# Attention head loop: one head more of lookahead, with a third buffer for scores and probabilities

## The chip, the cores and the metric

The kernel runs on the 8 cores of one Trainium2 chip, each core with its own batch element. The metric is the device time in microseconds of the slowest core, as the median of timed runs.

## The reference

One transformer layer on x of shape (8, 2048, 1024) in float32; one batch element of 2048 rows goes to each core. The attention is local: rows are taken in blocks of 64, and each block attends to itself alone, with 8 heads of 128.

```python
q = (src @ Wq + bq).reshape(B, nb, bs, H, dk)      # nb = 32 blocks of bs = 64
k = (src @ Wk + bk).reshape(B, nb, bs, H, dk)
v = (src @ Wv + bv).reshape(B, nb, bs, H, dk)
scores = jnp.einsum('bnqhd,bnkhd->bhnqk', q, k) * dk ** (-0.5)
probs = jax.nn.softmax(scores, axis=-1)
out = jnp.einsum('bhnqk,bnkhd->bnqhd', probs, v).reshape(B, S, D)
x = x + (out @ Wo + bo)                            # src is layernorm(x)
h = jnp.square(jax.nn.relu(jnp.einsum('bsd,fd->bsf', layernorm(x), W_fc)))
y = jnp.einsum('bsf,df->bsd', h, W_proj)           # then 5 spike steps, added to x
```

## The kernel before

The program is written out by hand: `plan` holds a list of instructions for each engine, in the order in which the Python code appends them, and each engine runs its list in that order. A wait stands in the list ahead of the instruction that needs it and holds back all that is behind it on that engine.

The attention runs in four passes (p = 0 to 3, called first to fourth) over 512 rows each. A pass has three parts. First come the projections: TensorE makes q and k (lines 336 and 356, evicted by ScalarE) and v (line 375, evicted by VectorE at line 383). Then comes the head loop, and last the output projection (line 617), with the residual added on VectorE (line 636) and the transposes of the next pass's normalized rows between.

In the head loop one step h (0 to 7) belongs to one head, that is 8 blocks of 64 rows. A head goes through these functions:

- `scores(h)`: 8 small matmuls into half h % 2 of psC (TensorE, line 405).
- `softmax_pre(h)`: maximum and subtraction from psC into s_f32 (VectorE, lines 419 and 422).
- `exp_h(h)`: exponential in place (ScalarE, line 431).
- `softmax_post(h)`: sum, reciprocal and product into p_bf (VectorE, lines 441, 444, 447).
- `pt_h(h)`: two transposes of p_bf into half h % 2 of psD (TensorE, line 459).
- `ptev_h(h)`: copy of them into pt_bf (ScalarE, line 468).
- `pv_h(h)`: probabilities times v into psA or psB (TensorE, line 488).
- `attnev_h(h)`: eviction with bias into attn_sb (VectorE, line 506).

Behind each head's PV the same loop transposes the FFN weights, which the second half of the kernel reads back from memory. `w2_group` makes 8 transposes of W2 into half 0 of psD (line 541), VectorE copies them to w2stage buffer 0 (line 551), and SP stores them to w2scratch (line 561). `w1_group` makes 8 transposes of W1 into half 1 of psD (line 514), ScalarE copies them to w2stage buffer 1 (line 525) and issues the store to w1scratch (line 533). So each of the two streams has one stage buffer and waits, ahead of a copy, for its own store of the step before. GpSimd refills the W2 buffers with 512 KB (line 197) behind every odd step's W2 transposes, and a W1 buffer with 256 KB (line 218) behind the W1 transposes of each step. In steps 1 to 4 of passes one to three ScalarE also computes the sums for the next pass's layer norm (lines 246 and 250), in step 5 VectorE and ScalarE turn them into a scale, and in step 6 VectorE applies it (line 283).

psD is shared: `relD` holds for each half the eviction that must be over before the next writer may start. The last passes' ends are followed by the FFN (lines 815 and 849) in eight tiles of 256 rows.

The order of the loop before:

```python
for h in range(8):
    if h + 2 < 8:
        E_s = scores(h + 2); softmax_pre(h + 2, E_s); exp_h(h + 2)
    if h + 1 < 8:
        softmax_post(h + 1); pt_h(h + 1); ptev_h(h + 1)
    pv_h(h)
    attnev_h(h)
    ...
    w2_group(ci, h % 2)
    ...
    w1_group(fcw)
```

Ahead of it stand scores, softmax_pre and exp of heads 0 and 1, and softmax_post, pt and ptev of head 0.

Of the kernel before, what the change touches and what calls it, by code (L numbers as in the profile page):

```python
# [12 lines left out]
ACT = mybir.ActivationFunctionType  # L13
# [11 lines left out]
def build_nc():  # L25
# [36 lines left out]
             for i in range(2)]  # L62
    p_bf = [e(nc.sbuf_tensor(f"p_bf_{i}", [128, 256], BF16, side="right"))
            for i in range(2)]
    pt_bf = [e(nc.sbuf_tensor(f"pt_bf_{i}", [128, 256], BF16, side="right"))
             for i in range(2)]
    ident = e(nc.sbuf_tensor("ident", [128, 128], BF16, side="right"))
# [252 lines left out]
    for p in range(PA):  # L320
# [93 lines left out]
        def softmax_pre(h, E_s):  # L414
            sv = psC[:, (h % 2) * 512:(h % 2) * 512 + 256]
            g3 = sv.rearrange("p (g k) -> p g k", g=4)
            wait("ve", "pe", E_s)
            wait("ve", "ve", war["tta"])
            op("ve", lambda E, g3=g3: E.tensor_reduce(
                negmax[:, :4], g3, AX.X, ALU.max, negate=True), inc="ve")  # L420
            wait("ve", "ve", n["ve"])
            op("ve", lambda E, h=h, g3=g3: E.tensor_tensor(
                s_f32[h % 2][:].rearrange("p (g k) -> p g k", g=4), g3,
                negmax[:, :4].unsqueeze(2).broadcast_to([128, 4, 64]),
                ALU.add), inc="ve")
            E_tta[h] = n["ve"]
            war["tta"] = n["ve"]

        def exp_h(h):
            wait("se", "ve", E_tta[h])  # L430
            op("se", lambda E, h=h: E.activation(
                s_f32[h % 2][:], s_f32[h % 2][:], ACT.Exp), inc="se")
            E_exph[h] = n["se"]

        def softmax_post(h):
            wait("ve", "se", E_exph[h])
            wait("ve", "ve", war["p"])
            if h >= 2:
                wait("ve", "pe", E_pt[h - 2])
            g3 = s_f32[h % 2][:].rearrange("p (g k) -> p g k", g=4)  # L440
# [7 lines left out]
                p_bf[h % 2][:].rearrange("p (g k) -> p g k", g=4), g3,  # L448
# [5 lines left out]
        def pt_h(h):  # L454
# [3 lines left out]
            for t_ in range(2):  # L458
                op("pe", lambda E, h=h, t_=t_, base=base: E.transpose(  # L459
                    psD[:, base + t_ * 128:base + (t_ + 1) * 128],  # L460
                    p_bf[h % 2][:, t_ * 128:(t_ + 1) * 128], ident[:]),
# [3 lines left out]
        def ptev_h(h):  # L465
# [3 lines left out]
                pt_bf[h % 2][:], psD[:, base:base + 256]), inc="se")  # L469
# [3 lines left out]
        def pv_h(h):  # L473
# [7 lines left out]
            for bl in range(8):  # L481
# [11 lines left out]
                       pt_bf[h % 2][kb:kb + 64,  # L493
# [82 lines left out]
        ptev_h(0)  # L576
        for h in range(8):
            if h + 2 < 8:
                E_s = scores(h + 2)
                softmax_pre(h + 2, E_s)  # L580
                exp_h(h + 2)
            if h + 1 < 8:
                softmax_post(h + 1)
                pt_h(h + 1)
                ptev_h(h + 1)
# [419 lines left out]
```

How the kernel before makes its waits and increments, by code:

```python
    def wait(eng, sem, val):  # L117
        if val <= 0:
            return
        assert val <= n[sem], (eng, sem, val, n[sem])
        emit(eng, lambda E, sem=sem, val=val: E.wait_ge(S[sem], val))
# [1 line left out]
    def op(eng, build, inc=None):  # L123
        if inc is None:
            emit(eng, lambda E, b=build: b(E))
            return None
        n[inc] += 1
        emit(eng, lambda E, b=build, s=inc: b(E).then_inc(S[s], 1))
        return n[inc]
# [3 lines left out]
    def dma(eng, build):  # L133
        npool = {"sy": NSY, "gp": NGP, "se": NSE}[eng]
        pfx = {"sy": "qs", "gp": "qg", "se": "qe"}[eng]
        k = qidx[eng] % npool
        qidx[eng] += 1
        nm = f"{pfx}{k}"
        if n[nm] > 0:
            wait(eng, nm, n[nm])
        n[nm] += 16
        emit(eng, lambda E, b=build, nm=nm: b(E).then_inc(S[nm], 16))
        return (nm, n[nm])
```

## Time and profile before

| | us |
|---|---|
| median of the timed runs (2 runs) | 1159.28 |
| lowest and highest of them | 1158.76, 1159.81 |
| profiled execution, its own time | 1154.09 |
| its span on the slowest core | 1152.5 |
| spans of the 8 cores | 1140.6 to 1152.5 |
| busy in the span: TensorE, VectorE, ScalarE, GpSimd | 831.0, 491.6, 411.8, 254.6 |

The span runs from the first to the last instruction of the slowest core. The head loops of the four passes begin at 99, 222, 347 and 470 us and end, with the first output projection matmul, at 158, 283, 407 and 523 us; the FFN fills the span from about 540 us on. A busy share is an average over both halves of the kernel and does not tell what a change in the head loop is worth.

### The profile page before, as it was taken

What the parts mean: (1) busy time and instruction counts of PE and PEld (TensorE: products, weight loads), DVE (VectorE), ACT (ScalarE), POOL (GpSimd) and SP (SyncE); (2) the same over time, 40 slices, a digit from 0 to 9 for tenths busy, and PEclk for the clock granted to TensorE, in tenths of its full rate; (3) what the DMA queues carried; (4) which work ended last, traced back from release to release, by engine and by line L of the source; (5) the groups of instructions that cost most, each with busy time, mean ns of one, the idle gap of its engine ahead of it and who ended that gap; (6) DMA issues with size and microseconds to landing.
All of it is one profiled execution on the core that took longest, in us unless ns stands there. A gap on an engine that the chain in (4) does not pass through costs nothing.

```text
span 1152.5 us, 19231 instructions; the slowest of 8 cores (1140.6 to 1152.5 us)
## 1 busy us (share of the span) xinstructions
PE 831.0 (72%) x6624; PEld 602.7 (52%) x6624; DVE 491.6 (43%) x561; ACT 411.8 (36%) x873; POOL 254.6 (22%) x122
## 2 busy tenths in 40 slices
PE   0196379744993389537897979879798897979910
PEld 0143234332442334323786868768587686867800
DVE  0105430343115430544005739275491845739186
ACT  3131523142223413121444444444444444454400
POOL 3000000011000100000003516153261633516154
PEclk9997569955996589758898999989899999999955
DMA  9994760067005730266586959779596996959700
GB/s 159 202 232 88 150 120 0 1 123 150 20 1 94 128 72 1 39 129 199 161 282 201 304 167 321 231 236 321 183 316 190 294 309 195 318 179 326 227 37 37
DMA packets 127292, 194.21 MB, mean 169 GB/s; under 512 B 42208, under 2 KB 44256, under 8 KB 127200
## 3 DMA queue, kind: packets, MB, share of 16 engines
q1 hardware_dynamic: 108144, 151.03, 43.3%
q0 software_dynamic: 14448, 33.56, 16.2%
q10 hardware_dynamic: 4608, 8.39, 2.0%
q8 instruction: 58, 0.95, 0.4%
q14 instruction: 34, 0.28, 0.1%
HBM read 192.95 MB, written 25.17 MB: 189 GB/s over the span
## 4 chain that ended last, share of the span: by engine, by line
PE 58%; DMA 18%; DVE 9%; ACT 6%; issue 5%; SPq 1%; POOL 1%; DVEq 0%; ACTq 0%; POOLq 0%
PE psC L815 16%; PE psA L849 9%; PE psB L849 8%; DMA w1slab<-w1scratch 7%; DMA w2scratch<-w2stage 5%; DMA bv_sb<-bv 3%; PE psA L617 3%; DMA w1scratch<-w2stage 3%; PE psA L336 3%; PE psB L617 2%; PE psB L375 2%; PE psA L375 2%; PE psB L356 2%; PE psA L356 2%; PE psB L336 2%
## 5 line engine op out<-in xcount | busy, mean ns | idle before, releaser
L815 PE MATMUL psC<-xn2t_sb,w1slab 128*128 128x256 bf16 x2048 | 274.1, 279 | 18.4 <-DMA w1slab<-w1scratch 9.7
L815 PEld LDWEIGHTS psC<-xn2t_sb,w1slab 128*128 128x128 bf16 x2048 | 203.6, 100 | 49.6 <-issue 22.1
L826 ACT ACTIVATE h_bf<-psC 128x256 bf16<-128x256 f32 x256 | 97.8, 382 | 223.5 <-PE psC L815 223.5
L849 PE MATMUL psA<-h_bf,w2slab 128*128 128x256 bf16 x1024 | 155.2, 274 | 25.5 <-ACT h_bf L829 22.4
L916 POOL TENSOR_TENSOR acc_q<-acc_q,spk_q 128x2048 bf16<-128x2048 bf16 (+1 forms) x27 | 148.4, 5495 | 72.4 <-DVE spk_q L912 72.4
L849 PE MATMUL psB<-h_bf,w2slab 128*128 128x256 bf16 x1024 | 154.3, 273 | 0.0
L920 DVE SCALAR_TENSOR_TENSOR mem_q<-mem_q,y_sb 128x2048 f32<-128x2048 f32 (+1 forms) x27 | 142.8, 5291 | 2.8
L849 PEld LDWEIGHTS psA<-h_bf,w2slab 128*128 128x128 bf16 x1024 | 98.6, 98 | 45.3 <-issue 33.6
L829 ACT ACTIVATE h_bf<-h_bf 128x256 bf16<-128x256 bf16 x256 | 106.6, 416 | 24.8 <-ACT h_bf L826 1.5
L849 PEld LDWEIGHTS psB<-h_bf,w2slab 128*128 128x128 bf16 x1024 | 100.7, 98 | 12.2
L218 POOL DMA_DIRECT2D wtmp<-Wfc x32 | 17.2, 539 | 387.6 <-PE psC L405 348.0
L459 PE MATMUL psD<-ident,p_bf 128*128 128x128 bf16 x64 | 11.5, 280 | 117.4 <-DVE p_bf L447 105.6
L383 DVE CAST v_bf<-psA 128x512 bf16<-128x512 f32 x16 | 11.1, 692 | 139.8 <-PE psA L375 139.8
L459 PEld LDWEIGHTS psD<-ident,p_bf 128*128 128x128 bf16 x64 | 4.3, 103 | 121.2 <-issue 121.2
L525 ACT COPY w2stage<-psD 128x1024 bf16<-128x1024 bf16 x32 | 32.4, 1012 | 96.7 <-DMA w1scratch<-w2stage 69.9
L712 DVE TENSOR_SCALAR nmean<-sums 128x1 f32<-128x1 f32 x16 | 2.5, 154 | 143.9 <-ACT xn_bf L705 143.5
L907 POOL COPY acc_q<-spk_q 128x2048 bf16<-128x2048 bf16 (+1 forms) x9 | 31.5, 3504 | 116.7 <-DVE spk_q L901 116.4
L918 DVE SCALAR_TENSOR_TENSOR mem_q<-mem_q,spk_q 128x2048 f32<-128x2048 f32 (+1 forms) x27 | 55.5, 2055 | 2.8
L795 POOL DMA_DIRECT2D out<-x_sb x16 | 9.4, 587 | 202.3 <-DVE x_sb L791 200.8
L791 DVE SCALAR_TENSOR_TENSOR x_sb<-psD,x_sb 128x1024 f32<-128x1024 bf16 x16 | 19.6, 1225 | 74.5 <-PE psD L783 74.4
L783 PE MATMUL psD<-ident,acc_q 128*128 128x128 bf16 x128 | 10.5, 230 | 53.9 <-POOL acc_q L930 43.5
L551 DVE COPY w2stage<-psD 128x1024 bf16<-128x1024 bf16 x32 | 22.1, 691 | 62.1 <-DMA w2scratch<-w2stage 49.7
(98 smaller groups left out, 1044.2 us busy)
## 6 DMA issues: line engine op xcount, KB each, us to landing
w2slab<-w2scratch SPq DMA_DIRECT2D x128, 512.0 KB, 7.1
w1slab<-w1scratch SPq DMA_DIRECT2D x128, 512.0 KB, 8.2
x_sb<-x SPq DMA_DIRECT2D x4, 2048.0 KB, 43.8
wtmp<-Wpr POOLq DMA_DIRECT2D x16, 512.0 KB, 6.5
wtmp<-Wfc POOLq DMA_DIRECT2D x32, 256.0 KB, 7.2
w2scratch<-w2stage SPq DMA_DIRECT2D x32, 256.0 KB, 4.5
w1scratch<-w2stage ACTq DMA_DIRECT2D x32, 256.0 KB, 4.9
out<-x_sb POOLq DMA_DIRECT2D x16, 512.0 KB, 7.6
```

The costliest lines, as they stand in the source:

```text
L336: op("pe", lambda E, oc=oc, c=c, qb=qb: E.matmul(qb, wq_sb[:, c * 1024 + oc * 128:c * 1024 + (oc + 1) * 128], xn1t_sb[:, c * 512:(c + 1) * ...
L356: op("pe", lambda E, oc=oc, c=c, qb=qb: E.matmul(qb, wk_sb[:, c * 1024 + oc * 128:c * 1024 + (oc + 1) * 128], xn1t_sb[:, c * 512:(c + 1) * ...
L375: op("pe", lambda E, jj=jj, half=half, c=c, qb=qb: E.matmul(qb, xn1t_sb[:, c * 512 + jj * 128:c * 512 + (jj + 1) * 128], wv_sb[:, c * 1024 ...
L525: op("se", lambda E, half=half, s=w2g["gidx"] % 2: E.copy(w2stage[s][:], psD[:, half * 1024:half * 1024 + 1024]), inc="se")
L617: E.matmul(pair[:, half * 512:(half + 1) * 512], attn_sb[:, c * 512 + jj * 128: c * 512 + (jj + 1) * 128], wo_sb[:, c * 1024 + half * 512: ...
L815: op("pe", lambda E, fc=fc, c=c, hp=hp, s1b=s1b: E.matmul(hp, s1b[:, c * 128:(c + 1) * 128], xn2t_sb[:, c * 256:(c + 1) * 256], start=(c = ...
L826: op("se", lambda E, fc=fc, hp=hp: E.activation(h_bf[fc % 2][:], hp, ACT.Relu), inc="se")
L829: op("se", lambda E, fc=fc: E.activation(h_bf[fc % 2][:], h_bf[fc % 2][:], ACT.Square), inc="se")
L849: E.matmul(tgt[:, mc * 256:(mc + 1) * 256], slb[:, m * 128:(m + 1) * 128], h_bf[fp % 2][:], start=(fp == 0 and m % 2 == 0), stop=(fp == 31 ...
L916: op("gp", lambda E, sv=sv, av=av: E.tensor_add(av, av, sv), inc="gp")
L918: vop(lambda E, sv=sv, mv=mv: E.scalar_tensor_tensor(mv, mv, 0.9, sv, ALU.mult, ALU.subtract))
L920: vop(lambda E, yv=yv, mv=mv: E.scalar_tensor_tensor(mv, mv, 1.0, yv, ALU.mult, ALU.add))
```

## The change

The three buffer sets s_f32, p_bf and pt_bf get three buffers each instead of two, and are indexed with h % 3. The loop works one head further ahead: step h makes scores, maximum, subtraction and exponential of head h+3 (before: h+2), and the second half of the softmax, transpose and eviction of head h+2 (before: h+1). The first head more of both is made ahead of the loop. psC and psD keep two halves, indexed with h % 2.

```diff
--- before.py
+++ after.py
@@ -59,11 +59,11 @@
     v_bf = regC.enter_context(nc.sbuf_tensor("v_bf", [128, 4096], BF16))
     attn_sb = regC.enter_context(nc.sbuf_tensor("attn_sb", [128, 4096], BF16))
     s_f32 = [e(nc.sbuf_tensor(f"s_f32_{i}", [128, 256], F32, side="right"))
-             for i in range(2)]
+             for i in range(3)]
     p_bf = [e(nc.sbuf_tensor(f"p_bf_{i}", [128, 256], BF16, side="right"))
-            for i in range(2)]
+            for i in range(3)]
     pt_bf = [e(nc.sbuf_tensor(f"pt_bf_{i}", [128, 256], BF16, side="right"))
-             for i in range(2)]
+             for i in range(3)]
     ident = e(nc.sbuf_tensor("ident", [128, 128], BF16, side="right"))
     wtmp2 = [e(nc.sbuf_tensor(f"wtmp2_{i}", [128, 2048], BF16, side="right"))
              for i in range(2)]
@@ -420,7 +420,7 @@
                 negmax[:, :4], g3, AX.X, ALU.max, negate=True), inc="ve")
             wait("ve", "ve", n["ve"])
             op("ve", lambda E, h=h, g3=g3: E.tensor_tensor(
-                s_f32[h % 2][:].rearrange("p (g k) -> p g k", g=4), g3,
+                s_f32[h % 3][:].rearrange("p (g k) -> p g k", g=4), g3,
                 negmax[:, :4].unsqueeze(2).broadcast_to([128, 4, 64]),
                 ALU.add), inc="ve")
             E_tta[h] = n["ve"]
@@ -429,15 +429,15 @@
         def exp_h(h):
             wait("se", "ve", E_tta[h])
             op("se", lambda E, h=h: E.activation(
-                s_f32[h % 2][:], s_f32[h % 2][:], ACT.Exp), inc="se")
+                s_f32[h % 3][:], s_f32[h % 3][:], ACT.Exp), inc="se")
             E_exph[h] = n["se"]
 
         def softmax_post(h):
             wait("ve", "se", E_exph[h])
             wait("ve", "ve", war["p"])
-            if h >= 2:
-                wait("ve", "pe", E_pt[h - 2])
-            g3 = s_f32[h % 2][:].rearrange("p (g k) -> p g k", g=4)
+            if h >= 3:
+                wait("ve", "pe", E_pt[h - 3])
+            g3 = s_f32[h % 3][:].rearrange("p (g k) -> p g k", g=4)
             op("ve", lambda E, g3=g3: E.tensor_reduce(
                 ssum[:, :4], g3, AX.X, ALU.add), inc="ve")
             wait("ve", "ve", n["ve"])
@@ -445,7 +445,7 @@
                inc="ve")
             wait("ve", "ve", n["ve"])
             op("ve", lambda E, h=h, g3=g3: E.tensor_tensor(
-                p_bf[h % 2][:].rearrange("p (g k) -> p g k", g=4), g3,
+                p_bf[h % 3][:].rearrange("p (g k) -> p g k", g=4), g3,
                 rsum[:, :4].unsqueeze(2).broadcast_to([128, 4, 64]),
                 ALU.mult), inc="ve")
             E_p[h] = n["ve"]
@@ -458,7 +458,7 @@
             for t_ in range(2):
                 op("pe", lambda E, h=h, t_=t_, base=base: E.transpose(
                     psD[:, base + t_ * 128:base + (t_ + 1) * 128],
-                    p_bf[h % 2][:, t_ * 128:(t_ + 1) * 128], ident[:]),
+                    p_bf[h % 3][:, t_ * 128:(t_ + 1) * 128], ident[:]),
                     inc="pe" if t_ == 1 else None)
             E_pt[h] = n["pe"]
 
@@ -466,7 +466,7 @@
             wait("se", "pe", E_pt[h])
             base = (h % 2) * 1024
             op("se", lambda E, h=h, base=base: E.copy(
-                pt_bf[h % 2][:], psD[:, base:base + 256]), inc="se")
+                pt_bf[h % 3][:], psD[:, base:base + 256]), inc="se")
             E_ptev[h] = n["se"]
             relD[h % 2] = ("se", n["se"])
 
@@ -490,7 +490,7 @@
                        v_bf[(bl % 2) * 64:(bl % 2) * 64 + 64,
                             (bl // 2) * 1024 + h * 128:
                             (bl // 2) * 1024 + (h + 1) * 128],
-                       pt_bf[h % 2][kb:kb + 64,
+                       pt_bf[h % 3][kb:kb + 64,
                                     tt * 128 + qc:tt * 128 + qc + 64],
                        start=True, stop=True),
                     inc="pe" if bl == 7 else None)
@@ -574,15 +574,21 @@
         softmax_post(0)
         pt_h(0)
         ptev_h(0)
+        E_s2 = scores(2)
+        softmax_pre(2, E_s2)
+        exp_h(2)
+        softmax_post(1)
+        pt_h(1)
+        ptev_h(1)
         for h in range(8):
+            if h + 3 < 8:
+                E_s = scores(h + 3)
+                softmax_pre(h + 3, E_s)
+                exp_h(h + 3)
             if h + 2 < 8:
-                E_s = scores(h + 2)
-                softmax_pre(h + 2, E_s)
-                exp_h(h + 2)
-            if h + 1 < 8:
-                softmax_post(h + 1)
-                pt_h(h + 1)
-                ptev_h(h + 1)
+                softmax_post(h + 2)
+                pt_h(h + 2)
+                ptev_h(h + 2)
             pv_h(h)
             attnev_h(h)
             ci = 4 * p + h // 2
```

On TensorE, ahead of step 0 of each pass, one pair of scores (line 405) and p_bf transposes (line 459) is added in front of the first PV (line 488):

```order
 L405 MATMUL psC<-k_bf,q_bf 64x64 x8
 L459 MATMUL psD<-ident,p_bf 128x128 x2
+L405 MATMUL psC<-k_bf,q_bf 64x64 x8
+L459 MATMUL psD<-ident,p_bf 128x128 x2
 L488 MATMUL psA<-pt_bf,v_bf 128x64 x8
 L541 MATMUL psD<-ident,wtmp_0 128x128 x8
```

The first W2 transposes (line 541) of a pass now stand behind three pairs, where they stood behind two (the first pair's scores come together with the ones before).

On TensorE, in steps 5 and 6 of each pass, the scores leave step 5 and the p_bf transposes leave step 6:

```order
 L541 MATMUL psD<-ident,wtmp_0 128x128 x8
 L514 MATMUL psD<-ident,wtmp_0 128x128 x8
-L405 MATMUL psC<-k_bf,q_bf 64x64 x8
 L459 MATMUL psD<-ident,p_bf 128x128 x2
 L488 MATMUL psB<-pt_bf,v_bf 128x64 x8
 L541 MATMUL psD<-ident,wtmp_0 128x128 x8
 L514 MATMUL psD<-ident,wtmp_1 128x128 x8
-L459 MATMUL psD<-ident,p_bf 128x128 x2
 L488 MATMUL psA<-pt_bf,v_bf 128x64 x8
 L541 MATMUL psD<-ident,wtmp_1 128x128 x8
```

Steps 0 to 4 keep the same row of kinds of instruction. On VectorE, step 2 before (s_f_0 and s_f_1 are the s_f32 buffers; head 4's maximum and subtraction, then head 3's sum, reciprocal and product):

```order
L419 TENSOR_REDUCE negmax<-psC 128x4
L422 TENSOR_TENSOR s_f_0<-psC,negmax 128x256
L441 TENSOR_REDUCE ssum<-s_f_1 128x4
L444 RECIPROCAL rsum<-ssum 128x4
L447 TENSOR_TENSOR p_bf<-s_f_1,rsum 128x256
L506 TENSOR_SCALAR attn_sb<-psA,bv_sb 128x2x4x64
L551 COPY w2stage<-psD 128x1024
```

and step 2 now (head 5's, then head 4's):

```order
L419 TENSOR_REDUCE negmax<-psC 128x4
L422 TENSOR_TENSOR s_f_2<-psC,negmax 128x256
L441 TENSOR_REDUCE ssum<-s_f_1 128x4
L444 RECIPROCAL rsum<-ssum 128x4
L447 TENSOR_TENSOR p_bf<-s_f_1,rsum 128x256
L506 TENSOR_SCALAR attn_sb<-psA,bv_sb 128x2x4x64
L551 COPY w2stage<-psD 128x1024
```

The heads moved by one, the order of the operations did not.

## Rows read from the trace of the kernel before

**Rows 1.** Totals by line, out<-in xcount, busy, mean ns, idle before and releaser.

```profile
L459 PE MATMUL psD<-ident,p_bf 128*128 128x128 bf16 x64 | 11.5, 280 | 117.4 <-DVE p_bf L447 105.6
```

**Rows 2.** Chain of waits from 221 to 284 us, second pass, shares by line.

```profile
by line: DMA w2scratch<-w2stage 29.7%; issue 13.0%; DMA w1scratch<-w2stage 11.9%; PE psD L541 6.4%; DVE negmax L419 3.4%; DVE w2stage L551 3.4%; ACT w2stage L525 3.2%; DVE xn_bf L283 3.2%; DVE p_bf L447 2.8%; PE psD L514 2.7%; DVE ssum L441
```

**Rows 3.** Timeline, second pass, steps 2 to 5: start us, us, engine, line.

```profile
244.56 0.53 POOL L218 DMA_DIRECT2D wtmp<-Wfc  x1 [6.06 <-PE psC L405]
...
247.20 0.69 DVE L551 COPY w2stage<-psD 128x1024 bf16<-128x1024 bf16 x1 [5.37 <-DMA w2scratch<-w2stage]
...
251.58 1.01 PE L541 MATMUL psD<-ident,wtmp 128*128 128x128 bf16 x8 [0.74 <-ACT pt_bf L468]
...
252.77 0.69 DVE L551 COPY w2stage<-psD 128x1024 bf16<-128x1024 bf16 x1 [1.06 <-PE psD L541]
...
262.79 0.69 DVE L551 COPY w2stage<-psD 128x1024 bf16<-128x1024 bf16 x1 [4.87 <-DMA w2scratch<-w2stage]
...
263.39 0.41 DVE L419 TENSOR_REDUCE negmax<-psC 128x4 f32<-128x256 f32 x1
...
264.25 0.41 DVE L441 TENSOR_REDUCE ssum<-s_f 128x4 f32<-128x256 f32 x1
...
265.73 0.37 PE L459 MATMUL psD<-ident,p_bf 128*128 128x128 bf16 x2 [6.14 <-DVE p_bf L447]
...
266.90 1.01 PE L541 MATMUL psD<-ident,wtmp 128*128 128x128 bf16 x8 [0.48 <-ACT pt_bf L468]
...
268.09 0.69 DVE L551 COPY w2stage<-psD 128x1024 bf16<-128x1024 bf16 x1 [0.80 <-PE psD L541]
```

**Rows 4.** DMA issues, last figure us to landing: step 4, step 3, first pass step 2.

```profile
w2scratch<-w2stage SPq DMA_DIRECT2D x1, 256.0 KB, 3.2
...
wtmp<-Wpr POOLq DMA_DIRECT2D x1, 512.0 KB, 6.5
...
w2scratch<-w2stage SPq DMA_DIRECT2D x1, 256.0 KB, 9.1
...
w2scratch<-w2stage SPq DMA_DIRECT2D x1, 256.0 KB, 5.2
```

**Rows 5.** Timeline, second pass, ahead of step 0 and steps 0 and 1.

```profile
225.86 0.27 PE L459 MATMUL psD<-ident,p_bf 128*128 128x128 bf16 x2 [3.71 <-DVE p_bf L447]
...
228.94 0.37 PE L459 MATMUL psD<-ident,p_bf 128*128 128x128 bf16 x2 [2.52 <-DVE p_bf L447]
...
230.94 0.69 DVE L551 COPY w2stage<-psD 128x1024 bf16<-128x1024 bf16 x1 [0.28 <-PE psD L541]
...
236.69 0.69 DVE L551 COPY w2stage<-psD 128x1024 bf16<-128x1024 bf16 x1 [0.48 <-PE psD L541]
```

**Rows 6.** Timeline, first pass: ahead of step 0, and steps 2, 3 and 5.

```profile
103.19 0.27 PE L459 MATMUL psD<-ident,p_bf 128*128 128x128 bf16 x2 [3.71 <-DVE p_bf L447]
...
106.80 0.37 PE L459 MATMUL psD<-ident,p_bf 128*128 128x128 bf16 x2 [2.94 <-DVE p_bf L447]
...
123.44 0.53 POOL L218 DMA_DIRECT2D wtmp<-Wfc  x1 [7.19 <-PE psC L405]
...
127.73 1.01 PE L541 MATMUL psD<-ident,wtmp 128*128 128x128 bf16 x8 [0.86 <-ACT pt_bf L468]
...
129.30 0.69 DVE L551 COPY w2stage<-psD 128x1024 bf16<-128x1024 bf16 x1 [1.56 <-DMA w2scratch<-w2stage]
...
143.00 1.01 PE L541 MATMUL psD<-ident,wtmp 128*128 128x128 bf16 x8 [0.41 <-ACT pt_bf L468]
```

**Rows 7.** Timeline, third pass step 5; fourth pass steps 5 and 6.

```profile
391.73 1.01 PE L541 MATMUL psD<-ident,wtmp 128*128 128x128 bf16 x8 [0.72 <-ACT pt_bf L468]
...
515.39 1.01 PE L541 MATMUL psD<-ident,wtmp 128*128 128x128 bf16 x8 [0.28 <-ACT pt_bf L468]
...
516.58 0.69 DVE L551 COPY w2stage<-psD 128x1024 bf16<-128x1024 bf16 x1 [0.60 <-PE psD L541]
...
520.50 0.69 DVE L551 COPY w2stage<-psD 128x1024 bf16<-128x1024 bf16 x1 [0.28 <-PE psD L541]
```

## The prediction

> **What bounds the kernel now.** I read first the totals by line, to see which waits in the attention part are large; then one attention pass in the chain of waits, to see which of them end last; then its timeline, row by row; and last the landing times of the stores, which the chain names.
>
> The totals point at the softmax: TensorE sits idle 105.6 us in front of the transposes of p_bf, 27 times, waiting for VectorE's p_bf [rows 1]. That idle time is what a deeper lookahead would be after. But a wait only tells who came last, not what set the pace. The chain of waits through the second pass's head loop names something else: DMA stores of the transposed FFN weights hold 29.7% and 11.9% of it, and p_bf 2.8% [rows 2]. So what counts is when each piece of work may start, not how busy an engine is.
>
> The timeline shows the rhythm. Each of the eight steps h ends with VectorE's copy of eight transposed W2 blocks into w2stage (line 551), then a store; there is one such stage buffer for W2, so the copy of step h waits for the store of step h-1. From step 3's copy to step 4's it is 252.77 to 262.79, 10.0 us, and the copy had waited 4.87 us for the DMA; from step 4's to step 5's it is 262.79 to 268.09, 5.3 us, and there it waited for TensorE's transposes [rows 3]. The store explains it: the one issued in step 4 lands in 3.2 us, the one of step 3 in 9.1 us, since the 512 KB load of the next W2 rows, issued beside it, takes 6.5 us on the same DMA engines [rows 4]. Steps 2, 4 and 6 are therefore paced by a slow store and hide whatever TensorE and VectorE do; steps 1, 3 and 5 are paced by the chain copy, softmax, transpose of p_bf, P times V, W2 transposes, copy; step 0 and what stands ahead of it are paced by that chain too.
>
> **What the change does to the waits.** In the loop, step h now makes scores(h+3), then the second half of the softmax of h+2, instead of h+2 and h+1. The order on VectorE is unchanged in kind: the maximum and the subtraction of the newest head, then sum, reciprocal and product of the one before it. TensorE's transpose of p_bf still stands right behind the scores just issued, so it still waits for those five VectorE operations. The exponential of a head is still issued one step ahead of its use, as before. What really gets a whole step more room is one edge: PV(h) now needs a pt_bf made two steps ago. That edge was never waited for: in the list of waits no PV (line 488) waits for pt_bf, which was made a whole step earlier; so it is worth nothing. A third buffer of s_f32, p_bf and pt_bf moves no data and costs nothing by itself.
>
> **Cost: one more softmax round ahead of step 0.** Scores(2)/softmax(1) come before the loop, and scores(3)/softmax(2) now precede the first W2 transposes. A round lasts, transpose to transpose, from 225.86 to 228.94, 3.08 us, in the second pass [rows 5], and from 103.19 to 106.80, 3.61 us, in the first [rows 6]. Nothing lies beside it: no store is under way, and TensorE stands idle 2.52 us of it. I count 3.61 + 3 x 3.08 = 12.85 us in full.
>
> **Gain: the round taken away at the end.** Step 6 has no round any more, and step 5 only the second half. In passes one to three step 6 waited for a slow store anyway, so its round was free, and taking it away gives 0. In step 5 the maximum and subtraction go: from 263.39 to 264.25, 0.86 us [rows 3]. In the fourth pass no loads are left and step 6's copy comes 3.92 us after step 5's [rows 7]; without the round it would wait for step 5's store, and 3.2 us of landing [rows 4] with the 0.9 us told below are no less. I take 0 there as well; a faster store could give some tenths.
>
> **Gain: the halves of psD change places.** The p_bf transposes of an odd step used half 0 of psD, which the W2 transposes behind them use as well; these had to wait until ScalarE had copied pt_bf out, 0.74 us in step 3 and 0.48 us in step 5 of the second pass [rows 3]. Now odd steps use half 1 and that wait goes to the W1 transposes, off the chain. Over the four passes it is 0.86, 0.74, 0.28 and 0.29 us in step 3 and 0.41, 0.48, 0.72 and 0.28 us in step 5 [rows 3, 6, 7] (of the three waits of 0.28 or 0.29 us one row stands). The 0.86 gives nothing, since that copy then waited for the DMA [rows 6]; step 3 gains 1.3 us. In step 1 it is about 0.2 us, which step 0 now pays in its turn, because even steps get the wait: the two cancel. In steps 2 and 4 the new wait (up to 1.2 us where ScalarE is at layer norm) hides behind the slow store, with 4.87 us of slack in step 4.
>
> Step 5 gains 0.86 and its wait, 1.27, 1.34, 1.58 and 1.14 us. Its gap of 5.30 us would shrink to 3.96 in the second pass, but the store puts a floor: copy 0.69, landing 3.2 [rows 4], and the time from the copy's end to the issue and from the landing to the next copy, which is what is left of 252.77 to 262.79 behind a copy of 0.69 and a landing of 9.1, 0.23 us [rows 3, 4]. Together 4.1 us. That takes off a bit over 0.1 us in each pass: 4.8 us in all.
>
> **The sum.** 12.85 - 1.3 - 4.8 = +6.7 us. The profiled execution took 1154.09 us (span 1152.5); it would become 1160.8. It lies 5.2 us or 0.4% below the median of the timed runs, 1159.28; set on that median the sum gives 1166.0 us. What comes after the loop (output projection, FFN) is only moved by this. Ends: if the store floor did not bind and all of steps 3 and 5 counted, the gains grow by 1.3 us; if the extra round cost only TensorE's idle time in it, 2.94 and three times 2.52 us [rows 5, 6], it falls by 2.35 us; the sum is then +3. The upper end is the third rival's.
>
> **The page on gaps.** A rule speaks for the change. The Trainium skill, Perfetto Trace Analysis, section Optimization Strategy, says that the same gap repeating on an engine can mean too few buffers for the next tile. By it three buffers would close the gap of 2.5 us and more ahead of the p_bf transposes. This case's rows put another cause there: the wait ends with a VectorE operation that starts only after scores of the same step, and it would with any number of buffers.
>
> **Rivals.** First, *the lookahead works*: the p_bf transposes no longer wait. For it: the 105.6 us. Against it: the order of instructions just told. Its price is read from the odd steps: from the first VectorE operation after the copy to the transpose is 263.39 to 265.73, 2.34 us [rows 3], 3 steps in 4 passes, 28 us; with the round ahead of the loop paid it is 1159.3 - 28.1 + 12.85 = 1144 us; were that round hidden as well, 1131 us.
>
> Second, *a wash*: each pass gains as much as it pays, because something downstream absorbs the round. Against it: ahead of step 0 no store or load is pending that could absorb it. It would give 1159 us.
>
> Third, *slower stores*, on the slower side. In even steps the W2 and W1 transposes now stand behind the pt_bf copy, so W1's refill, issued behind the W1 transposes, starts about 1 us later and overlaps more with the even step's fast store. That this matters is seen in step 2 of the first pass: the refill was issued at 123.44, less than 1 us ahead of the store, the store took 5.2 us to land instead of 3.2, and the next copy waited 1.56 us for it [rows 4, 6]. At a landing of L the odd gaps become L + 0.92, against 5.75 in step 1 (230.94 to 236.69 [rows 5]), 4.9 in step 3 (5.57 [rows 3] less the wait) and 4.1 in step 5: 4 x (3L - 12.0) us more. With L = 5.2 that is 14 us, 1180 us in all. The point from which it is over 2% (23.2 us, about what a measurement of this kernel can tell from no change) is L = 5.4; at L = 6.0 it is 24 us, 1190 us. Against it: in step 2 of the second pass the refill was issued at 244.56, over 3 us ahead of the store behind the copy of 247.20 [rows 3], so a shift of 1 us leaves it ahead. The Trainium skill, DMA: Bandwidth & Descriptors, section Issuing engines are not separate DMA queues, says that transfers of all issuing engines interleave on the same 16 DMA engines. This trace agrees: 9.1 us beside a load, 3.2 without one [rows 4].
>
> **Chances.** Forecast (between 1155 and 1174, centre 1166.0): 0.83. Stores slower, up to 1182: 0.06; beyond 2% slower: 0.03. Lookahead works in part or in full, below 1155: 0.08, of which more than 2% faster 0.02. The wash lies inside the forecast's range. The range 1155 to 1175 takes the sum's lower end of +3 with a scatter of 0.4%, as between the profiled execution and the timed ones, and half of the third rival. Within 2% is then 0.95.
>
> **What would show it.** Right: in every pass the first w2stage copy comes 3.1 us later behind the first scores; p_bf waits stay near 100 us in total; the gap from copy 4 to copy 5 is near 4.1 us and ends on a DMA; gaps from odd to even copies stay near 10 us; W2 transposes of odd steps no longer wait for pt_bf. Wrong: if the total of p_bf waits falls by half, if the time from the first scores of a pass to its output projection gets shorter, or if even steps' stores land in over 5 us.

## The result, and the profile after

The changed kernel takes 1167.85 us as the median of 11 runs, against 1157.03 us for the kernel before, as the median of 10 runs of the same sessions. The ratio is 1.0098, with a 95% interval from 1.0078 to 1.0118: about 11 us slower (9 to 14), within 2%. Both medians include a few runs in which the cores of one die ran at a lower granted clock (the slowest took 1274.91 us); the ratio leaves these out. The profiled execution's span is 1164.1 us on its slowest core, which is core 1; the mean of the eight cores' spans went from 1147.8 to 1155.9 us.

The total of the waits in front of the p_bf transposes, from the totals by line of the profile after (core 1, its slowest; [rows 1] are of core 0, the slowest before), in the same columns:

```profile
L459 PE MATMUL psD<-ident,p_bf 128*128 128x128 bf16 x64 | 11.5, 280 | 104.0 <-DVE p_bf L447 99.7
```

On the same core it is 103.8 us before and 99.7 us after (core 1), 105.6 and 104.2 us (core 0). The longer lookahead left nearly all of it in place.

The timeline of core 0 after, ahead of step 0 and in steps 0 and 1 of the second pass, answers to [rows 5] (start us, us, engine, line, and in brackets the idle time before and what ended it):

```profile
222.35 0.47 PE L405 MATMUL psC<-k_bf,q_bf 128*64 128x64 bf16 x16
...
226.53 0.27 PE L459 MATMUL psD<-ident,p_bf 128*128 128x128 bf16 x2 [3.71 <-DVE p_bf L447]
...
229.60 0.37 PE L459 MATMUL psD<-ident,p_bf 128*128 128x128 bf16 x2 [2.52 <-DVE p_bf L447]
...
232.96 0.37 PE L459 MATMUL psD<-ident,p_bf 128*128 128x128 bf16 x2 [2.62 <-DVE p_bf L447]
...
233.94 1.01 PE L541 MATMUL psD<-ident,wtmp 128*128 128x128 bf16 x8 [0.25 <-ACT pt_bf L468]
...
235.13 0.69 DVE L551 COPY w2stage<-psD 128x1024 bf16<-128x1024 bf16 x1 [0.57 <-PE psD L541]
...
240.62 0.69 DVE L551 COPY w2stage<-psD 128x1024 bf16<-128x1024 bf16 x1 [0.28 <-PE psD L541]
```

There are three p_bf transposes before the first W2 transposes, where there were two. The added round lasts from 229.60 to 232.96, 3.36 us. The W2 transposes of step 0 now wait 0.25 us for pt_bf; those of step 1 no longer wait, and the gap to the second copy is 5.49 us, where it was 5.75. The first copy comes 12.8 us behind the first scores.

The same core and pass in steps 2 to 5, to be held against [rows 3]:

```profile
249.51 0.53 POOL L218 DMA_DIRECT2D wtmp<-Wfc  x1 [7.08 <-PE psC L405]
...
250.63 0.69 DVE L551 COPY w2stage<-psD 128x1024 bf16<-128x1024 bf16 x1 [4.82 <-DMA w2scratch<-w2stage]
...
254.49 1.04 PE L541 MATMUL psD<-ident,wtmp 128*128 128x128 bf16 x8
...
257.01 0.69 DVE L551 COPY w2stage<-psD 128x1024 bf16<-128x1024 bf16 x1 [1.59 <-DMA w2scratch<-w2stage]
...
266.04 0.69 DVE L551 COPY w2stage<-psD 128x1024 bf16<-128x1024 bf16 x1 [4.53 <-DMA w2scratch<-w2stage]
...
271.25 0.69 DVE L551 COPY w2stage<-psD 128x1024 bf16<-128x1024 bf16 x1 [1.56 <-DMA w2scratch<-w2stage]
```

The W2 transposes of step 3 no longer wait for pt_bf, as forecast. But it brings nothing in step 3 and next to nothing in step 5: the copies of steps 3 and 5 now end their wait on a DMA, after 1.59 and 1.56 us, where they had waited for TensorE, and the two gaps are 6.38 and 5.21 us, where they were 5.57 and 5.30. The DMA issues of this step 2 say why; the last figure is the time to landing:

```profile
w1scratch<-w2stage ACTq DMA_DIRECT2D x1, 256.0 KB, 4.9
w2scratch<-w2stage SPq DMA_DIRECT2D x1, 256.0 KB, 5.5
```

The W1 refill was issued at 249.51 us, only 1.1 us ahead of the copy; before, it was 244.56 against 247.20, 2.6 us ahead [rows 3].

One core and one pass scatter, so the comparison rests on all cores. The table gives the distances between the starts of the W2 copies (line 551), read off the timelines, as the mean of the eight cores of the profiled execution, added up over the four passes, in us. Its columns for the experiments belong to the next section.

| from, to | before | after | halves | paired | late | late, 2 | stage 4 | stage 4, after |
|---|---|---|---|---|---|---|---|---|
| first scores, copy 0 | 37.1 | 51.9 | 50.9 | 51.7 | 44.5 | 31.1 | 37.4 | 51.8 |
| copy 0, copy 1 | 23.1 | 22.0 | 23.1 | 22.0 | 27.3 | 29.3 | 23.0 | 22.0 |
| copy 1, copy 2 | 39.6 | 39.5 | 39.9 | 45.0 | 27.5 | 27.6 | 21.8 | 25.9 |
| copy 2, copy 3 | 21.6 | 22.1 | 21.8 | 19.6 | 19.7 | 22.9 | 27.3 | 22.4 |
| copy 3, copy 4 | 39.2 | 36.4 | 38.6 | 42.8 | 34.5 | 31.5 | 22.1 | 25.9 |
| copy 4, copy 5 | 21.2 | 19.8 | 19.9 | 16.8 | 16.8 | 19.4 | 26.9 | 16.5 |
| copy 5, copy 6 | 33.9 | 33.4 | 36.0 | 35.3 | 35.0 | 30.5 | 24.1 | 18.9 |
| copy 6, output projection | 16.6 | 17.0 | 17.4 | 17.2 | 16.2 | 19.8 | 20.5 | 16.9 |
| head loops, sum | 232.3 | 242.2 | 247.6 | 250.3 | 221.4 | 212.1 | 202.9 | 200.4 |

The head loops became 9.9 us longer, which is the change in time within its interval. 14.8 us were lost ahead of copy 0, and 4.9 us came back behind it.

### The profile page after: what moved, and what is told of

The parts are those of the page before. It is cut to its first block, busy times and chain, and to the rows that moved or that the text cites. A ratio compares the mean times of both kernels' runs of the same rounds, so it can differ in the third digit from the quotient of the medians.

```text
span 1164.1 us, 19227 instructions; the slowest of 8 cores (1146.0 to 1164.1 us)
## 1 busy us (share of the span) xinstructions
PE 835.2 (72%) x6624; PEld 604.1 (52%) x6624; DVE 491.1 (42%) x561; ACT 411.8 (35%) x873; POOL 251.9 (22%) x122
## 4 chain that ended last, share of the span: by engine, by line
PE 59%; DMA 18%; DVE 9%; ACT 5%; issue 5%; SPq 1%; POOL 1%; DVEq 0%; ACTq 0%; POOLq 0%
PE psC L821 16%; PE psA L855 9%; PE psB L855 8%; DMA w2scratch<-w2stage 8%; DMA w1slab<-w1scratch 5%; PE psA L623 3%; DMA bv_sb<-bv 3%; PE psA L336 3%; PE psB L623 2%; PE psB L375 2%; PE psA L375 2%; PE psB L356 2%; PE psA L356 2%; PE psB L336 2%; DMA w1scratch<-w2stage 2%
## 5 line engine op out<-in xcount | busy, mean ns | idle before, releaser
L926 DVE SCALAR_TENSOR_TENSOR mem_q<-mem_q,y_sb 128x2048 f32<-128x2048 f32 (+1 forms) x27 | 139.2, 5155 | 2.8
L459 PE MATMUL psD<-ident,p_bf 128*128 128x128 bf16 x64 | 11.5, 280 | 104.0 <-DVE p_bf L447 99.7
L541 PE MATMUL psD<-ident,wtmp 128*128 128x128 bf16 x256 | 32.3, 304 | 41.5 <-DVE w2stage L551 26.4
L924 DVE SCALAR_TENSOR_TENSOR mem_q<-mem_q,spk_q 128x2048 f32<-128x2048 f32 (+1 forms) x27 | 59.1, 2189 | 3.2 <-DVE spk_q L918 0.5
L913 POOL COPY acc_q<-spk_q 128x2048 bf16<-128x2048 bf16 (+1 forms) x9 | 31.5, 3504 | 116.8 <-DVE spk_q L907 116.6
L551 DVE COPY w2stage<-psD 128x1024 bf16<-128x1024 bf16 x32 | 22.1, 691 | 74.4 <-DMA w2scratch<-w2stage 69.3
L797 DVE SCALAR_TENSOR_TENSOR x_sb<-psD,x_sb 128x1024 f32<-128x1024 bf16 x16 | 19.6, 1225 | 74.2 <-PE psD L789 74.0
```

The lines of the kernel that those rows point to most:

```text
L924: vop(lambda E, sv=sv, mv=mv: E.scalar_tensor_tensor(mv, mv, 0.9, sv, ALU.mult, ALU.subtract))
L926: vop(lambda E, yv=yv, mv=mv: E.scalar_tensor_tensor(mv, mv, 1.0, yv, ALU.mult, ALU.add))
```

## The experiments

Every kernel was compared with the kernel before, run in the same session; its ratio is given with the 95% interval.

**The buffers alone** (e1_buffers_only). The kernel before, with this part of the change only:

```diff
 s_f32, p_bf, pt_bf:
-             for i in range(2)]
+             for i in range(3)]
 and every s_f32[h % 2], p_bf[h % 2], pt_bf[h % 2]:
-                s_f32[h % 2]
+                s_f32[h % 3]
-            if h >= 2:
-                wait("ve", "pe", E_pt[h - 2])
+            if h >= 3:
+                wait("ve", "pe", E_pt[h - 3])
```

> The kernel before with three buffers for s_f32, p_bf and pt_bf (indexed h % 3) and the old order of the loop. Theory (the order costs, the buffers cost nothing): within 2 us of before, all gaps of the head loop as before. Rival (the third buffers, or the tensors that they shift in SBUF, cost or bring something by themselves): a good part of the changed kernel's +11 us, 5 us or more.

Measured: 1.0001 (0.9985 to 1.0017), head loops 232.6 us in the sum of the table. The buffers cost nothing that can be measured; all of the change's time is in its order.

**The halves of psD changed back** (e2_swap_halves, column "halves").

```diff
 def pt_h and ptev_h of the changed kernel:
-            pe_wait_rel(relD[h % 2])
-            base = (h % 2) * 1024
+            pe_wait_rel(relD[(h + 1) % 2])
+            base = ((h + 1) % 2) * 1024
-            relD[h % 2] = ("se", n["se"])
+            relD[(h + 1) % 2] = ("se", n["se"])
```

> The changed kernel, but the p_bf transposes of head h use the other half of psD, so that each step meets the half that it met before. It tells the cost of the swapped halves from that of the round ahead of step 0. Theory (the round, about 13 us, is the cost; the swapped halves bring a little in steps 3 and 5 and give it back where the W1 refill comes 1 us later and the even steps' store lands later): the first copy still comes 3.4 us later per pass, W1 refills of even steps go out 1 us earlier, copies of step 3 wait for a DMA as seldom as before, in all +8 to +12 us over before. Rival (the late refill is what made it slower than the sum): 5 us or more faster than the changed kernel, at +6 us or less over before.

Measured: 1.0146 (1.0127 to 1.0166), 17 us over before and outside the range that I gave. Neither side was right in size, and the rival fell with its sign: the swapped halves are a net gain of the change, 5.4 us in the head loops (247.6 against 242.2). The gain does not lie where the prediction had put it. The gaps of steps 3 and 5 are the same with either half (21.8 and 19.9 us here, 22.1 and 19.8 in the changed kernel); 4.8 of the 5.4 us lie in the slow gaps behind copies 3 and 5. With the refill less late (in step 2 it goes out 2.1 to 3.7 us ahead of the store on the mean of a pass, in the changed kernel 1.2 to 3.1) the store of step 2 lands in 3.2 to 4.5 us, against 3.6 to 5.1 in the changed kernel. The extra round stays: copy 0 comes 13.7 us later than before, over the four passes.

**The weight transposes one step earlier**, in the changed kernel (e3_after_early) and in the kernel before (e4_before_early).

```diff
         softmax_pre(1, E_s1)
         exp_h(1)
+        weights(0)        # w2_group and w1_group of step 0
 for h in range(8):
...
-            w2_group(ci, h % 2)
...
-            w1_group(fcw)
+            if h + 1 < 8:
+                weights(h + 1)
```

> The changed kernel with the weight transposes of each step moved one step ahead: those of step 0 stand behind scores(1), so that the first stores run beside the softmax rounds ahead of the loop, and step 7 has none. Theory (the extra round costs because no store runs beside it): the first copy comes some 3 us behind the first scores instead of 13, the extra round is hidden, and the kernel is 8 us or more faster than before, and within 4 us of the same move made to the kernel before. Rival (the longer lookahead costs by itself, wherever the stores stand): it stays 8 us or more slower than the same move made to the kernel before.

> The kernel before with the same move of the weight transposes one step ahead. Theory (a chain of eight stores in each pass sets the pace, and what stands ahead of the first of them is exposed): the first copy comes some 6 us earlier in each pass, 15 to 25 us faster than before. Rival (VectorE's and TensorE's softmax rounds set the pace, the stores only fill the gaps): no faster than before by more than 5 us.

Measured: the move made to the kernel before gives 1.0019 (1.0003 to 1.0035), made to the changed kernel 1.0119 (1.0097 to 1.0140). My theory failed here twice. In e4 the first copy comes 2.7 us behind the first scores instead of 9.3, 26 us earlier over the four passes, and nothing is left of it. The distance from copy 0 to copy 1 grew by 6.6 us in all, since two softmax rounds now stand in it, and the way from copy 6 to the output projection by 24.4 us. The timeline of VectorE in core 0 of e4, end of the second pass, shows that way:

```profile
274.42 0.69 DVE L551 COPY w2stage<-psD 128x1024 bf16<-128x1024 bf16 x1 [5.87 <-DMA w2scratch<-w2stage]
...
277.39 0.42 DVE L447 TENSOR_TENSOR p_bf<-s_f,rsum 128x256 bf16<-128x256 f32 x1
278.89 0.75 DVE L506 TENSOR_SCALAR attn_sb<-psA,bv_sb 128x512 bf16<-128x512 f32 x1 [1.07 <-PE psA L488]
279.91 0.69 DVE L551 COPY w2stage<-psD 128x1024 bf16<-128x1024 bf16 x1 [0.28 <-PE psD L541]
282.20 2.98 DVE L283 TENSOR_SCALAR xn_bf<-x_sb,nmean,rstd 128x1024 bf16<-128x1024 f32 x4 [1.60 <-ACT w2stage L525]
285.10 0.75 DVE L506 TENSOR_SCALAR attn_sb<-psB,bv_sb 128x512 bf16<-128x512 f32 x1
```

Before, the last slow store (that of step 5) hid the last head's softmax, and the copy of step 7 stood behind the last eviction. Now copy 6, which waits for that store, belongs to step 5, and behind it a softmax, two PVs, a further copy and the layer norm follow in the open. The three slow gaps themselves did not move (38.8, 39.4 and 33.6 us in the sum of the passes, before 39.6, 39.2 and 33.9). So I read that it is not the start of the stores that counts but how much of the softmax lies beside a slow store: a pass has three of these (the fourth pass two), whenever they start, and whatever is not beside one of them is added to its time. And e3 stays 12 us behind e4 in the head loops (245.5 against 233.6): the rival was right that the order of the change costs wherever the stores stand, as long as they are slow. Its gap from copy 0 to copy 1 is 14.0 us longer in the sum of the passes, which is the extra round again, and its end 5.4 us shorter.

**The refills kept away from the even steps' stores** (e11_refill_paired, column "paired").

```diff
 def w1_group(fc) of the changed kernel:
-            if fc + 4 < 32:
+            if fc % 2 == 1 and fc + 3 < 32:
+                w1_dma(fc + 3)
                 w1_dma(fc + 4)
```

> The changed kernel, but an even step's W1 refill is issued together with the next odd step's, so that no load runs beside the even steps' stores. Theory (the gains of steps 3 and 5 were given back because the refill, some 2.4 us instead of 3.5 us ahead of the store, made that store land in 4 to 5 us): stores of steps 2 and 4 land in under 3.2 us, the gaps of steps 3 and 5 fall to the 4.8 and 4.1 us of the prediction; the slow stores get up to 1 us slower from the second refill; in all 2 to 6 us faster than the changed kernel. Rival (the gaps of 5 us have another cause, such as ScalarE's queue): gaps of steps 3 and 5 stay at 5.2 to 5.8 us in the first three passes.

Measured: 1.0158 (1.0143 to 1.0173). The step that I wanted to test behaved nearly as expected: the stores of steps 2 and 4 landed in 2.6 to 2.9 us on the mean of a pass, but for step 4 of the third pass with 3.6, where they had taken 3.3 to 5.1 us in the changed kernel. Core 0, second pass, step 2's store:

```profile
w2scratch<-w2stage SPq DMA_DIRECT2D x1, 256.0 KB, 2.8
```

step 1's store there:

```profile
w2scratch<-w2stage SPq DMA_DIRECT2D x1, 256.0 KB, 10.5
```

and the copies of steps 1 to 5 in the timeline (line 552 is line 551 here):

```profile
240.52 0.69 DVE L552 COPY w2stage<-psD 128x1024 bf16<-128x1024 bf16 x1 [0.28 <-PE psD L542]
...
251.94 0.69 DVE L552 COPY w2stage<-psD 128x1024 bf16<-128x1024 bf16 x1 [6.27 <-DMA w2scratch<-w2stage]
...
256.99 0.69 DVE L552 COPY w2stage<-psD 128x1024 bf16<-128x1024 bf16 x1 [0.28 <-PE psD L542]
...
267.15 0.69 DVE L552 COPY w2stage<-psD 128x1024 bf16<-128x1024 bf16 x1 [5.01 <-DMA w2scratch<-w2stage]
...
271.09 0.69 DVE L552 COPY w2stage<-psD 128x1024 bf16<-128x1024 bf16 x1 [0.30 <-DMA w2scratch<-w2stage]
```

With the collision gone the step 5 gap is 3.94 us here and 4.2 on the mean of the passes, the step 3 gap 5.05 and 4.9: the prediction had 4.1 and 4.9. The rival fell. One remainder is open: in the third pass the step 5 gap is 5.0 us and the store of step 4 ahead of it takes 3.6, though no refill was issued in the 10 us ahead of it. But the time did not fall with it. The slow gaps grew, 1.4 to 1.6 us each: that from copy 1 to copy 2 by 5.5 us over the passes and that from copy 3 to copy 4 by 6.4 us, where I had allowed up to 1 us each. Step 1's store takes 10.5 us here, with two refills issued behind it.

**The p_bf transposes at the end of the step** in the changed kernel (e5_pt_late, column "late") and in the kernel before, with its two buffers and its lookahead of two heads (e9_before_pt_late, column "late, 2").

```diff
                 softmax_post(h + 2)
-                pt_h(h + 2)
-                ptev_h(h + 2)
             pv_h(h)
...
             w1_group(fcw)
+            if h + 2 < 8:
+                pt_h(h + 2)
+                ptev_h(h + 2)
```

> The changed kernel, but the p_bf transposes of head h+2 and their eviction stand behind the W1 transposes at the end of step h instead of ahead of PV(h). Theory (the lookahead only brings something where TensorE's transposes are moved away from the softmax that feeds them): W2 transposes no longer wait for the step's softmax, the first copy comes 3 us earlier in each pass than in the changed kernel, steps 3 and 5 fall to the store's floor of 4.1 to 5 us, in all 10 to 18 us faster than the changed kernel, so level with before or up to 7 us faster. Rival (the wait only moves: the late transposes wait for the copies of the same step, which wait for the slow store): within 5 us of the changed kernel or slower.

> The kernel before (two buffers, lookahead of two heads) with only the p_bf transposes of head h+1 and their eviction moved behind the W1 transposes of step h. It tells whether the late transposes need the third head of lookahead. Theory (what counts is where TensorE's transposes stand; the longer lookahead only adds the round ahead of step 0): faster than the same placement in the changed kernel by the exposed round, 5 to 12 us, so 15 to 22 us faster than before. Rival (with one step less, PV(h) waits for the pt_bf just made): level with it or slower.

Measured: 0.9913 (0.9888 to 0.9939) and 0.9839 (0.9820 to 0.9859). Moved away from the softmax that feeds them, the transposes stop holding up PV and the W2 transposes, and the changed kernel becomes 20.8 us shorter in its head loops, somewhat more than I had expected. Only part of that is the softmax wait itself. 12.0 of the 20.8 us lie between copy 1 and copy 2, a gap that a slow store paces: the W2 transposes of step 1 no longer stand behind that step's softmax, so the 512 KB load behind them goes out 4.2 us ahead of the store of step 1 instead of 0.4, and that store lands in 6.0 us instead of 9.0 (means of all cores and passes; in e9 4.0 and 6.0 us). The gap from copy 0 to copy 1 grows by 5.3 us instead. No run separates the two causes. The move needs none of the third head of lookahead: without it the same move is 9 us better still in the head loops; 13.4 us of that come ahead of copy 0 (31.1 against 44.5 us), and the steps behind give 4 back. The wait moved, too. The totals by line of e9 show VectorE's copy as the largest part of what the p_bf transposes now wait for, since they need the half of psD that it empties (39.3 us more are ScalarE's copy of W1, 14.8 us p_bf itself):

```profile
L459 PE MATMUL psD<-ident,p_bf 128*128 128x128 bf16 x64 | 11.6, 281 | 101.5 <-DVE w2stage L551 47.3
```

101.5 us of idle time in front of the line is nearly what the changed kernel has (104.0), and yet e9 is some 30 us faster than it, by the two ratios: the number of the idle time does not say what it costs.

**Four stage buffers**, so that a copy waits for the store of two steps before: in the kernel before (e6_before_stage4, column "stage 4"), with the changed order (e7_after_stage4, column "stage 4, after"; its s_f32 and p_bf have two buffers again, pt_bf three), and in the kernel before with the earlier transposes (e8_before_stage4_early).

```diff
 w2stage:
-                                side="right")) for i in range(2)]
+                                side="right")) for i in range(4)]
 in w1_group and w2_group:
-            if w2g["gidx"] >= 2:
-                wait("se", *E_st2[w2g["gidx"] - 2])
+            if w2g["gidx"] >= 4:
+                wait("se", *E_st2[w2g["gidx"] - 4])
-            s=w2g["gidx"] % 2
+            s=w2g["gidx"] % 4
```

> The kernel before with four w2stage buffers instead of two, so that a copy waits for the store of two steps before, not of the last step. Theory (three slow stores of 9.8 us in each pass set the pace of every other step): the gaps of steps 2, 4 and 6 fall from 9.8 us towards the 5.3 us of the others, head loops get 8 to 13 us shorter per pass, 25 to 45 us faster in all. Rival (DMA throughput, busy 61% of the head loops, or TensorE's and VectorE's chain set the pace): under 10 us faster.

> The changed order with the four w2stage buffers (s_f32 and p_bf with two buffers again, which its order needs no third of; pt_bf has three). Theory (no slow store hides a softmax round any more, so each of the eight rounds is exposed in both orders): the round ahead of step 0 is paid back by the round that leaves step 6, and the two orders lie within 4 us of each other. Rival (the order costs wherever the stores stand): it stays 8 us or more behind the old order with four buffers.

> The kernel before with four w2stage buffers and the weight transposes one step ahead. Theory: the transposes of step 0 fill TensorE's wait for the first softmax, but the last step's stand ahead of the output projection's input as in the variant without the extra buffers; within 5 us of the old order with four buffers. Rival (with the stores out of the way the early start is a net gain): 8 us or more faster than it.

Measured: 0.9724 (0.9703 to 0.9744), 0.9855 (0.9810 to 0.9901), 0.9782 (0.9756 to 0.9808).

In e6 hardly a copy waits for a store any more (7 of 256 over all cores), and the head loops lose 29 us. In e7 the two orders meet as expected, but only inside the head loops: 200.4 us with the changed order, 202.9 with the old. In whole time e7 is 17 us behind (1144.42 against 1127.68). Most of that difference sits between the head loops: from the output projection to the next pass's first scores it takes 69.0, 69.8 and 65.8 us (means of the cores), against 63.5, 63.4 and 63.4 in e6. The timeline of core 1 of e7, end of the second pass, shows where:

```profile
280.68 0.69 DVE L551 COPY w2stage<-psD 128x1024 bf16<-128x1024 bf16 x1 [9.94 <-DMA w2scratch<-w2stage]
281.29 1.28 DVE L642 SCALAR_TENSOR_TENSOR x_sb<-psA,x_sb 128x512 f32<-128x512 f32 x2
...
281.52 1.01 PE L302 MATMUL psD<-ident,xn_bf 128*128 128x128 bf16 x8 [3.72 <-DVE w2stage L551]
```

The last copy of the pass waits 9.94 us for a store. TensorE's transposes of the next pass's rows (line 302) need the half of psD which that copy empties, and the rest of the output projection stands behind them: they wait 3.72 us here, and 8.7 us in each core over the three passes that have a successor, in e6 nothing. Behind the wait the granted clock is 0.50 (1.2 GHz) from 281.5 to 286.4 us, where e6's core 1 has 1.00 (2.4 GHz) at the same place, from 273.4 to 278.1 us; I take this for the rest of the 14.2 us between the head loops, which no run tested. The changed order bunches its last steps (copies 4, 5 and 6 come at distances of 4 to 6 us), and the stores of steps 5 and 6 take 14 to 19 us to land in the first three passes; in e6 they take 4 to 10. That the bunching makes them slow is my reading. I had not seen this coming, and my expectation was wrong for the time. The rival was right in the number, for a reason it did not name. e8 is 7 us behind e6, a little more than expected: the rival fell.

**Both levers** (e10_stage4_pt_late): four stage buffers and the late p_bf transposes, in the kernel before.

> The kernel before with four w2stage buffers and the late p_bf transposes. Theory (two separate causes, the slow stores and the exposed softmax rounds): their gains add in part, 40 to 55 us faster than before. Rival (with the stores free, DMA throughput, 61% busy in head loops that were 30% longer, is the next limit): no faster than with four w2stage buffers alone.

Measured: 0.9582 (0.9550 to 0.9613), 1112.06 us, 47 us faster than before. The gains add in part, as expected, and the rival fell (e6 took 1127.68 us); the head loops take 185.2 us in sum. The busy shares of 222 to 262 us, in the second pass of all three (its head loop ends at 257 us in e10's core 0), show what comes next; the columns are the stretch, its length, busy time of TensorE, weight loads, VectorE, ScalarE and GpSimd with counts, the granted clock, the DMA share and GB/s. First the kernel before, then e6, then e10:

```profile
222.00:262.00 40.00, 15.67 (x189) 11.81 (x183) 18.41 (x42) 15.41 (x29) 3.69 (x7) 0.55 0.58 107
```

```profile
222.00:262.00 40.00, 19.35 (x215) 14.89 (x212) 20.82 (x47) 20.21 (x37) 5.83 (x11) 0.50 0.88 165
```

```profile
222.00:262.00 40.00, 21.04 (x190) 14.54 (x192) 18.98 (x43) 18.67 (x34) 5.27 (x9) 0.51 0.94 176
```

The DMA engines go from 58% to 88% and 94% busy (over the eight cores 50% to 66%, 78% to 88% and 86% to all of it). In e10 some copies wait for a store again, 35.3 us in core 3, where e6's core 3 has none. So e10 looks near a DMA limit, which no run tested; the kernel before was far from it.

## Why the prediction was right

It forecast 1166.0 us in a range from 1155 to 1175; 1167.85 was measured. Against a median before of 1157.03 in these sessions the change was +11 us, where the sum said +6.7. The direction and the main mechanism held; two terms of the sum were too kind, and a third effect, which the sum had at nothing, made up for part of that.

**The order of instructions keeps the wait.** Held. The p_bf waits went from 105.6 to 104.2 us on core 0 and from 103.8 to 99.7 us on core 1, e1 shows that the buffers are worth nothing, and e5 and e9 show that time is won when the transposes move, with or without the third head.

**The extra round, 12.85 us.** Mechanism right, a little too small. Ahead of copy 0 the loss is 14.8 us. I had booked the 0.25 us wait of step 0 against step 1, and step 1 did give back 1.1 us, which leaves 13.7. The rest is that a round is not 3.08 us everywhere: the added ones took 3.28, 3.31, 3.67 and 3.34 us (transpose to transpose, means of the cores). In the second pass the clock has a part in it. Between 229.60 and 233.00 us the granted clock is 0.50, which is 1.2 GHz, behind a first stretch at 1.00, which is 2.4 GHz; TensorE was busy 1.37 of the 7.1 us in the two stretches ahead of it. Profile of the changed kernel, core 0, the same columns as above:

```profile
222.00:226.00 4.00, 0.81 (x18) 0.35 (x16) 2.95 (x8) 0.83 (x2) 0.00 (x0) 1.00 0.00 0
226.50:229.60 3.10, 0.56 (x10) 0.40 (x11) 1.78 (x5) 0.79 (x2) 0.00 (x0) 0.66 0.00 0
229.60:233.00 3.40, 0.77 (x11) 0.48 (x12) 1.78 (x5) 0.79 (x2) 0.00 (x0) 0.50 0.00 0
```

The round that I took from the trace of before is the one that stands at 0.66 here, and took 3.08 us; the one added behind it runs wholly at the lower level, and took 3.36 us. The clock is not all: in the first pass both rounds of core 0 stand at 0.50 and take 3.68 and 3.28 us, and why the third pass's took 3.67 us is open.

**Nothing lost when step 6 loses its round.** Right in its core: its gap moved from 33.9 to 33.4 us, and in the fourth pass from 3.92 to 3.58, which is the few tenths spoken of.

**Steps 3 and 5, gains of 1.3 and 4.8 us.** This is the term that was mis-sized. Step 3 lost 0.6 us, step 5 gained 1.4. The edge did disappear as predicted, but I set the store's floor from a single landing of 3.2 us. On the mean of the cores the stores of steps 2 and 4 took 3.2 to 4.1 us already before; after, they took 3.6 to 5.1 us in step 2 (4.4 over the passes) and 3.3 to 4.5 us in step 4. That is the third rival, short of the 5.2 us from which it was priced, though in the third pass step 2's store, with 5.1 us, crosses the 5 us that I had named as a sign of being wrong. My argument against it failed: I held a refill harmless as long as it goes out ahead of the store. In step 2 it went out 3.1, 2.3, 1.7 and 1.2 us ahead (the fourth pass, then the first, second and third), and the store took 3.6, 4.2, 4.8 and 5.1 us. e11 shows that the collision with the W1 refill is the main cause: without it the step 3 gap is as I had worked it out, and the step 5 gap too, except in the third pass. And e2 shows that the changed places of the halves, from which I had all of step 3's gain and some 2 us of step 5's, bring nothing on balance in these two gaps; step 5's 1.4 us came with either half. In the fourth pass, where no W1 load is left for step 4, the step 5 gap was 4.17 us in the changed kernel itself; I had 4.1.

**Slow gaps stay near 10 us.** Not quite. Those from copy 3 to copy 4 fell by 2.8 us in sum. They take back part of what step 3 did not gain: W2's load is issued behind the transposes and no longer waits for what the copy waits for, so it has more of a start when the copy is late. I read this from the rows (transposes of step 3 at 254.49, copy at 257.01). The means agree: in step 3 the load goes out 0.5 us ahead of the store before and in e2, with 39.2 and 38.6 us from copy 3 to copy 4, and 1.0 us ahead in the changed kernel, with 36.4. No run tested it alone. Steps 3 to 6 together came out at -4.1 us, where the sum had -6.1.

**The rivals.** The lookahead as such did not work. The wash did not come. The slower stores came in part. The lower end of the sum, +3, rested on a round costing only TensorE's idle time, and that was wrong: it costs its whole length.

**Luck in the number.** The 1166.0 us lie closer to 1167.85 than the sum deserves. It was some 4 us short of the change, and stood on a median of 1159.28 where these sessions gave 1157.03. Within the head loops the gains of steps 3 and 5 were 5.2 us too large and the round 0.9 us too small, and the slow gap behind copy 3, which I had unchanged, gave 2.8 us back.

## What to carry to other kernels

A deeper lookahead removes a wait only if the order of each engine's queue lets the consumer run past the producer's newest work; moving the dependent transposes to the end of the step was worth 19 to 21 us, part of it because loads then went out earlier ahead of a slow store, while one head more of lookahead with the old placement cost 11. Before paying for a software-pipeline stage, count which of its rounds lie beside something slower, here three slow stores in each of the first three passes: a round taken out of such a shadow and put ahead of the loop is paid in full. And take the length of a transfer that sets a floor from the mean over cores and passes, not from one row.

## What the runs showed of the hardware

- A 256 KB store to w2scratch lands in 2.6 to 3.3 us where no load was issued in the 8 us ahead of it (step 0, and steps 4 to 7 of the fourth pass), in 3.3 to 5.1 us with a 256 KB refill issued 1.2 to 3.9 us ahead, and in 7.7 to 9.5 us beside a refill and a 512 KB load issued 0.4 to 2.3 us ahead (means of a pass over eight cores, before and after). With the load 4.0 to 4.3 us and the refill 3.2 to 3.5 us ahead of it, in e5's step 1, it took 5.4 to 6.4 us. In e7, where copies 4 to 6 come at 4 to 6 us, those of steps 5 and 6 took 14 to 19 us.
- Keeping a load out of one store's way puts it in another's: in e11 the stores of steps 2 and 4 gained 1.6 and 1.0 us and the slow gaps from copies 1 and 3 grew by 1.4 and 1.6 us each, and the kernel was 7 us slower than the changed one (ratios 1.0158 and 1.0098).
- The Trainium skill, DMA: Bandwidth & Descriptors, section Issuing engines are not separate DMA queues, has transfers from all engines interleave on the same 16 DMA engines. e11 agrees, with its stores of 2.8 and 10.5 us in one pass.
